# A ternary feed-forward's half chunk packed into one PSUM bank, its slot order, and matmuls put at the head of TensorE's queue, in a four-block float32 network on one core

## The chip, the cores and the metric

The kernel runs on one core of one Trainium2 chip. The metric is device microseconds of one execution. The three runs shown of the kernel before took 422.45, 421.94 and 420.12 us (median 421.94). The profiled execution took 420.34 us, of which the profile's span is 418.6 us.

## The reference

Four residual blocks over 8 sequences of 256 tokens and 256 channels, float32, with a layer norm behind each: a time-mixing recurrence (RWKV), a mixture of 8 experts of which each token takes 2, a linear attention with 16 heads, and a ternary feed-forward. The change touches the last one and the start of the first:

```python
def _quantize(w):                       # w1, w2: (704, 256), w3: (256, 704)
    gamma = jnp.mean(jnp.abs(w))
    return jnp.clip(jnp.round(w / (gamma + EPS)), -1.0, 1.0)
def _bitlinear(x, w): return jnp.matmul(x, _quantize(w).T)
x1 = _bitlinear(x, w1); x2 = _bitlinear(x, w2)
hidden = jax.nn.sigmoid(x1) * x2
return _bitlinear(hidden, w3)
# the first block
k = einsum(xk, Wk); v = einsum(xv, Wv); r = einsum(xr, Wr)
x = layernorm(x + L0_attn(x)); x = layernorm(x + L0_ffn(x))
x = layernorm(x + L1_attn(x)); x = layernorm(x + L1_ffn(x))
```

The hidden width of the last block is 704, which is five and a half chunks of 128.

## The kernel before, in words

All order is written out by hand: each engine has its own list of instructions and waits on semaphores for the others. There are three stages.

Stage A is the recurrence and the routing, sequence by sequence. SyncE issues the loads (`xs[0]`, then `vec`, then `Wk`, `Wv`, `Wr`). ScalarE (L794) and VectorE (L1048) scale the raw weights to `wA`; then TensorE's `project` makes keys, values and gates in float32, of which each instruction appears as two records in the trace (the key projection of a sequence is 8 instructions, 16 records). VectorE's memsets at the head end in `cleared`.

Stage B runs 39 tiles of 128 expert rows. Per tile TensorE does `turn_hidden`, `gate_up` of the tile after the next, `down`, `turn` (L547, L537, L558, L517); VectorE does `hidden_turned` (L1234), on which `down` waits, and `hidden` (L1228). Between them `prepare(i)` slips in one step of other work per tile: the sums of absolute weights (`wsum`, L1298 and L1302), the thresholds, and the quantising of W1, W2 (L1315, L1319) and W3 (L1327 to L1333). `w1q` and `w2q` are padded with zeros to six chunks, and so is `raw3`.

Stage C is attention and the feed-forward, in slots: slot s does the attention of sequence s and the feed-forward of sequence b = s - 1. TensorE's slot for s = 1 to 6 is: `keys_values(s)`, `turn_x3(b)`, `queries(s)`, `key_values(s)`, `ternary(b, 0)`, `attend(s)` (L719), `ternary(b, 1)`, `turn_an(s)`, `ternary_out(b, 0)`, `turn_x2(s+1)`, `ternary(b, 2)`, `attention_out(s)`, `ternary_out(b, 1)`, `ternary_out(b, 2)`. In slot 7 `attention_out` stands ahead of `ternary(b, 2)`, and slot 8 has the feed-forward of the last sequence alone.

A piece p of `ternary` is two chunks: eight matmuls with `w1q` into one bank and eight with `w2q` into another (per chunk two halves of the channels, each with `x3_hi` and `x3_lo`). Each piece then goes ScalarE `tanh_half` (L941), VectorE `gate_times` (L1409), ScalarE `f_high` (`fh`, the rounded high part, L780), VectorE `f_low` (`fl`, what is left, L1415), and back to TensorE's `ternary_out` (L664), eight matmuls into bank 7. Behind the last one VectorE's `block_out` (L1421) takes bank 7, and on the same queue follow its statistics, `combined(s+2)` (L1348, L1351), `keys` (L1426), `x3_low` (L1431), the query limits (L1437), `queries` (L1444) and `mask_kv` (L1450), on which `attend` waits. `attention_residual` (L1472) waits for `attention_out`; behind it come the statistics of `x3` (L1019), GpSimd's `deviation` and ScalarE's `normalise` (L785), for which the next slot's `turn_x3` waits.

## Time and profile before

| | |
|---|---|
| runs | 422.45, 421.94, 420.12 us, median 421.94 |
| the profiled execution | 420.34 us, span 418.6 us |
| TensorE matmuls busy | 378.5 us (90%), 2264 records |
| TensorE weight loads busy | 330.7 us (79%) |
| VectorE busy | 288.5 us (69%) |
| ScalarE busy | 205.2 us (49%) |
| GpSimd busy | 129.7 us (31%) |
| granted TensorE clock, mean | 0.967 |
| chain that ended last | PE 51%, DVE 25%, ACT 10%, issue 6%, POOL 5% |
| stage A / B / C | about 0 to 120 / 120 to 233 / 233 to 418.6 us |

PE is TensorE's matmuls, PEld its weight loads, DVE VectorE, ACT ScalarE, POOL GpSimd, SPq SyncE's queue. Matmuls overlap each other, so their busy time is longer than the time from one start to the next; the starts are to be read for their cost. The chain that ended last is followed back from the last instruction to what released it, or to the instruction before it on its engine. The names in the trace are those of the tiles without their numbers ("arena" is the one large scratch tile).

### The profile page before, as it was taken

The page shows a single profiled execution, that of the slowest core. Times are in us where ns is not written, and L with a number is a line of the kernel's source. Part 1 is how long each engine was busy: PE and PEld are TensorE (multiplying, and loading weights), DVE is VectorE, ACT ScalarE, POOL GpSimd, SP SyncE. Part 2 cuts the span into 40 slices and gives each one's busy share as a digit, 9 for nine tenths or more (in the row PEclk, how much of TensorE's full clock was granted, in tenths as well). Part 3 has the DMA queues.
Part 4 walks back from the last instruction along what each step waited for, and adds up shares of the span by engine and source line. Part 5 has one row for each costly group of instructions (what it writes and reads, how often), then busy time and mean ns, then how long its engine had stood idle before and what let it go on. Part 6 is the DMA issues. An engine that isn't in the chain of part 4 may idle for free.

```text
span 418.6 us, 7345 instructions
## 1 busy us (share of the span) xinstructions
PE 378.5 (90%) x2264; PEld 330.7 (79%) x2264; DVE 288.5 (69%) x756; ACT 205.2 (49%) x419; POOL 129.7 (31%) x228
## 2 busy tenths in 40 slices
PE   3999999999868999999999867999999999999781
PEld 3888888888747877777776757988999999999680
DVE  4697899999984554896453256686868686866531
ACT  3372785568554333355344414545546363646341
POOL 2002166445635500030310377152617131311111
PEclk9999999999978999999999969999999999999886
DMA  6444973421123457533521222101111000000000
GB/s 215 151 167 160 141 191 92 139 76 52 38 76 114 151 178 218 160 104 99 155 74 52 66 78 66 32 28 50 38 39 50 28 27 2 25 2 27 0 27 26
DMA packets 28487, 35.70 MB, mean 85 GB/s; under 512 B 3681, under 2 KB 25633, under 8 KB 28193
## 3 DMA queue, kind: packets, MB, share of 16 engines
q1 hardware_dynamic: 19760, 21.72, 18.3%
q0 software_dynamic: 3072, 8.39, 6.2%
q10 hardware_dynamic: 5616, 5.11, 3.5%
q8 instruction: 20, 0.33, 0.3%
q14 instruction: 19, 0.15, 0.1%
HBM read 22.76 MB, written 12.45 MB: 84 GB/s over the span
## 4 chain that ended last, share of the span: by engine, by line
PE 51%; DVE 25%; ACT 10%; issue 6%; POOL 5%; DMA 1%; SPq 0%; ACTq 0%; POOLq 0%; DVEq 0%
PE bank L394 20%; PE bank L537 11%; PE bank L558 8%; PE bank L664 4%; DVE st L1019 3%; POOL nm L1537 2%; PE bank L719 2%; PE bank L517 2%; PE bank L547 2%; PE bank L404 2%; DVE arena L1080 2%; DVE arena L1444 2%; DVE arena L1083 2%; DVE fl L1415 2%; POOL rs L1534 2%
## 5 line engine op out<-in xcount | busy, mean ns | idle before, releaser
L394 PE MATMUL bank<-arena 128*128 128x256 f32 (+2 forms) x576 | 119.4, 363 | 7.7 <-ACT arena L794 6.4
L394 PEld LDWEIGHTS bank<-arena 128*128 128x128 f32 x576 | 101.8, 194 | 21.5 <-issue 6.4
L780 ACT ACTIVATE arena<-bank 128x256 f32<-128x256 f32 (+1 forms) x118 | 45.4, 423 | 47.3 <-PE bank L558 27.7
L1532 POOL TENSOR_TENSOR ve<-mv,eps 128x2 f32<-128x2 f32 x32 | 7.2, 224 | 157.7 <-DVE mv L1023 157.6
L537 PE MATMUL bank<-gu,arena 128*128 x156 | 54.0, 469 | 0.0
L785 ACT ACTIVATE arena<-arena,nm,rs 128x256 f32<-128x256 f32 x48 | 26.2, 595 | 38.2 <-POOL nm L1537 38.0
L558 PE MATMUL bank<-dn,arena 96*128 x156 | 40.9, 384 | 2.8 <-DVE arena L1234 2.8
L1602 POOL DMA_INDIRECT arena<-yg,ypos x32 | 31.2, 976 | 38.9 <-DMA yg<-arena 30.5
L1234 DVE COPY arena<-bank 96x256 f32<-96x256 f32 x39 | 16.3, 419 | 35.0 <-PE bank L547 34.9
L1574 POOL DMA_INDIRECT xg<-x,pos x32 | 34.3, 1073 | 14.7 <-DVE pos L1143 7.4
L558 PEld LDWEIGHTS bank<-dn,arena 96*128 96x128 f32 x156 | 28.8, 190 | 12.2 <-issue 3.9
L537 PEld LDWEIGHTS bank<-gu,arena 128*128 128x128 f32 x156 | 27.1, 194 | 8.7 <-issue 0.7
L664 PE MATMUL bank<-w3q,fh 128*128 128x256 f32 x96 | 27.2, 315 | 5.2 <-DVE fl L1415 5.2
L1409 DVE SCALAR_TENSOR_TENSOR arena<-arena,bank 128x512 f32<-128x512 f32 x24 | 16.5, 688 | 18.5 <-ACT arena L941 18.5
L941 ACT ACTIVATE arena<-bank 128x512 f32<-128x512 f32 x24 | 14.3, 597 | 29.1 <-PE bank L394 29.1
L394 PE MATMUL bank<-x_hi,w1q 128*128 128x256 f32 x96 | 26.5, 308 | 1.6 <-ACT x_hi L780 1.6
L868 ACT ACTIVATE arena<-bank 128x176 f32<-128x176 f32 x39 | 12.3, 315 | 31.4 <-PE bank L537 31.4
L1537 POOL TENSOR_SCALAR nm<-mv,rs 128x1 f32<-128x1 f32 x64 | 23.8, 385 | 3.2
L1534 POOL TENSOR_TENSOR rs<-ve,neghalf 128x2 f32<-128x2 f32 x32 | 24.0, 751 | 2.5
L394 PE MATMUL bank<-x_lo,w1q 128*128 128x256 f32 x96 | 24.5, 287 | 0.0
L664 PE MATMUL bank<-w3q,fl 128*128 128x256 f32 x96 | 24.4, 286 | 0.0
L394 PE MATMUL bank<-x_hi,w2q 128*128 128x256 f32 x96 | 24.3, 285 | 0.0
(211 smaller groups left out, 855.5 us busy)
## 6 DMA issues: line engine op xcount, KB each, us to landing
arena<-xg SPq DMA_DIRECT2D x39, 128.0 KB, 2.2
yg<-arena ACTq DMA_DIRECT2D x39, 128.0 KB, 1.7
arena<-in_xT SPq DMA_DIRECT2D x8, 256.0 KB, 3.0
x<-in_x SPq DMA_DIRECT2D x8, 256.0 KB, 4.4
out<-arena SPq DMA_DIRECT2D x8, 256.0 KB, 2.1
gu<-in_w_gate SPq DMA_DIRECT2D x1, 1408.0 KB, 7.9
gu<-in_w_up SPq DMA_DIRECT2D x1, 1408.0 KB, 7.7
dn<-in_w_down SPq DMA_DIRECT2D x11, 128.0 KB, 6.1
```

The source lines that it names most:

```text
L394: last = pe.matmul(dst, l, r, start=i == 0, stop=i == len(pairs) - 1)
L537: last = pe.matmul(bank[BANK_GU[i % 2]][:, 0:2 * F], xtT[:, i % 2, chunk(k)], w[:, :, k, :, bass.ds(e, 1), :], start=k == 0, stop=k == KC - 1)
L558: last = pe.matmul(bank[BANK_Y][:, 0:C], hT[0:HALF, i % 2, q, :], dn[0:HALF, q, bass.ds(e, 1), :], start=q == 0, stop=q == 1)
L664: last = pe.matmul(halves(7)[:, t, :], l[:, n % 2, i, chunk(t)], w3q[:, f, :], start=f == 0 and t == 0 and q == 0, stop=f == NF - 1 and q ...
L780: return act.activation(dst, src, ACT.Copy)
L785: last = act.activation(dst[:, t, :], src[:, t, :], ACT.Identity, bias=nm[:, i, t:t + 1], scale=rs[:, i, t:t + 1])
L1234: dve.tensor_copy(hT[0:HALF, i % 2, :, :], bank[BANK_HT][0:HALF, 0:2 * P].rearrange("p (q t) -> p q t", q=2)).then_inc(hT_ok, 1)
L1409: dve.scalar_tensor_tensor(fb[n % 2][:, :, :], fb[n % 2][:, :, :], 1.0, halves(ternary_banks(b, p)[1]), ALU.add, ALU.mult).then_inc(fx_ok, 1)
L1534: pool.tensor_tensor(rs[:, i, :], ve[:, i, :], neghalf[:, :], ALU.pow).then_inc(dev_step, 1)
L1537: last = pool.tensor_scalar(nm[:, i, t:t + 1], mv[:, i, t, 0:1], rs[:, i, t:t + 1], -1.0, ALU.mult, ALU.mult)
L1574: pool.indirect_dma_start(out=xg, out_offset=bass.IndirectOffsetOnAxis(ap=pos[:, n, j:j + 1], axis=0), in_=x1[:, n, :], in_offset=None).th ...
L1602: pool.indirect_dma_start(out=yy[b % 2][:, t, j, :], out_offset=None, in_=source, in_offset=bass.IndirectOffsetOnAxis(ap=ypos[:, n, j:j + ...
```

## The change

- The last piece of `ternary` is split in two. The half chunk (64 gate columns of W1 and the 64 columns of W2 that belong to them) is packed in one set of 128 columns, chunk 5 of `w1q`: four matmuls into one bank (`HALF_PIECE`), where it took eight. Chunk 4 is the piece behind it (`LAST_PIECE`), eight matmuls. ScalarE's tanh of the half piece reads partitions 0 to 63 and writes 64 to 127; its low part is written to partitions 0 to 63 of `fh`, beside the high part, and W3's last 64 rows are loaded twice, so that `ternary_out` needs two matmuls for the half chunk, where it took four.
- The half piece goes to bank 2 (bank 4 for the last sequence) and waits for `gate_times` of piece 1; the last chunk's piece keeps banks 5 and 6.
- ScalarE does tanh, tanh, high, high and VectorE gate, gate, low, low for the two. On VectorE both `f_low` stand ahead of `attention_residual` in slots 1 to 6; before, `f_low` stood behind it.
- `ternary_out` of the half chunk waits for its own low part, and chunk 4 for its own.
- The quantising of W2 writes 640 columns to `w2q` and 64 to `w1q`; the sum over W3 is two instructions, of partitions 0 to 63 with six chunks and of 64 to 127 with five. The memsets of padding are gone.
- At the head: nine float32 matmuls of `ones` by `ones` once `cleared` is there; VectorE's memset of `ones` comes first; `Wk` is the first load on SyncE's queue and `vec` is loaded from ScalarE's.

The diff, cut to its core:

```diff
@@ ternary_banks @@
+    if p == HALF_PIECE:
+        return (4 if b == B - 1 else 2,)
+    return (0, 1) if p == LAST_PIECE and b == B - 1 else (5, 6)
@@ sync @@
+            sp.dma_start(raw_kvr[:, 0, :, :], chunked(Wk)).then_inc(in_kvr[0], 16)
             sp.dma_start(xs[0][:, :, 1:], xT_v[0]).then_inc(in_xsb[0], 16)
-            sp.dma_start(vec[:, :, :], vecs).then_inc(in_vec, 16)
-            for j, w in enumerate((Wk, Wv, Wr)):
+            for j, w in ((1, Wv), (2, Wr)):
@@ tensor @@
+            pe.wait_ge(cleared, 1)
+            for i in range(WARM):
+                pe.matmul(bank[7][:, 0:P], ones[:, :], ones[:, :], start=True, stop=True)
@@ ternary @@
-                past(pe, fx_ok, NPAIR * b + p - 1)
+                if p < HALF_PIECE:
+                    past(pe, fx_ok, PIECES * b)
+                if p == HALF_PIECE and b < B - 1:
+                    pe.wait_ge(fx_ok, PIECES * b + 2)
+                if p == LAST_PIECE and b < B - 1:
+                    pe.wait_ge(fx_ok, PIECES * b + 1)
@@ ternary_out @@
+                groups = [(PIECES * b + p + 1, [(2 * p, 0, (fh, fl)), (2 * p + 1, 1, (fh, fl))])] if p < NPAIR - 1 else [
+                    (PIECES * b + HALF_PIECE + 1, [(NF - 1, 1, (fh,))]),
+                    (PIECES * b + LAST_PIECE + 1, [(NF - 2, 0, (fh, fl))])]
@@ f_low @@
+                low, whole, high = {
+                    HALF_PIECE: (fh[0:LEFT, 0, 1, :], fb[0][LEFT:P, 1, :], fh[LEFT:P, 0, 1, :]),
+                    LAST_PIECE: (fl[:, 0, 0, :], fb[0][:, 0, :], fh[:, 0, 0, :]),
@@ vector, prepare @@
+                    for parts, n in ((slice(0, LEFT), NF), (slice(LEFT, P), NF - 1)):
+                        last = dve.tensor_reduce(wsum[parts, 2:3], raw3[parts, 0:n, :], mybir.AxisListType.XY, ALU.add,
@@ vector, c_slot @@
                 if ffn:
-                    gate_times(s - 1, 2)
+                    gate_times(s - 1, HALF_PIECE)
+                    gate_times(s - 1, LAST_PIECE)
+                    f_low(s - 1, HALF_PIECE)
+                    f_low(s - 1, LAST_PIECE)
                 if s < B - 1:
                     attention_residual(s)
-                if ffn:
-                    f_low(s - 1, 2)
```

TensorE's queue in slots 1 to 6, from the transposes of `turn_x2` to the first matmul of `attention_out` (bank 0). Before:

```order
L404 MATMUL bank4<-cst,arena 128x128 x4
L394 MATMUL bank5<-x3_hi,w1q 128x256
L394 MATMUL bank5<-x3_lo,w1q 128x256
...
L394 MATMUL bank6<-x3_hi,w2q 128x256
L394 MATMUL bank6<-x3_lo,w2q 128x256
...
L394 MATMUL bank0<-biases,pick 128x256
```

After:

```order
L410 MATMUL bank4<-cst,arena 128x128 x4
L400 MATMUL bank2<-x3_hi,w1q 128x256
L400 MATMUL bank2<-x3_lo,w1q 128x256
...
L400 MATMUL bank5<-x3_hi,w1q 128x256
L400 MATMUL bank5<-x3_lo,w1q 128x256
...
L400 MATMUL bank6<-x3_hi,w2q 128x256
L400 MATMUL bank6<-x3_lo,w2q 128x256
...
L400 MATMUL bank0<-biases,pick 128x256
```

There were eight matmuls into bank 5 and eight into bank 6; now there are four into bank 2, four into bank 5 and four into bank 6.

VectorE's queue in the same place (`arena<-arena,bank` is a gate, `fl<-arena,fh` a low part, `arena<-bank0,arena` the residual of attention). Before:

```order
L1415 TENSOR_TENSOR fl<-arena,fh 128x512
L1358 TENSOR_TENSOR xT_lo<-bank4,xT_hi 128x512
L1409 SCALAR_TENSOR_TENSOR arena<-arena,bank6 128x512
L1472 TENSOR_TENSOR arena<-bank0,arena 128x512
L1415 TENSOR_TENSOR fl<-arena,fh 128x512
L1019 BN_STATS st<-arena 128x6 x2
```

After:

```order
L1390 TENSOR_TENSOR xT_lo<-bank4,xT_hi 128x512
L1445 SCALAR_TENSOR_TENSOR arena<-arena,bank2 64x256
L1445 SCALAR_TENSOR_TENSOR arena<-arena,bank6 128x256
L1453 TENSOR_TENSOR fh<-arena,fh 64x256
L1453 TENSOR_TENSOR fl<-arena,fh 128x256
L1509 TENSOR_TENSOR arena<-bank0,arena 128x512
L1047 BN_STATS st<-arena 128x6 x2
```

One gate and one low part of 512 columns became two and two of 256, and all four stand ahead of the residual, which stood between them.

The head of SyncE's queue (`arena<-in_xT` is `xs`). Before:

```order
L315 DMA arena<-in_xT 128x2x256
L316 DMA vec<-in_vecs 128x12
L318 DMA raw_kvr<-in_Wk 128x2x256
L318 DMA raw_kvr<-in_Wv 128x2x256
L318 DMA raw_kvr<-in_Wr 128x2x256
```

After:

```order
L321 DMA raw_kvr<-in_Wk 128x2x256
L322 DMA arena<-in_xT 128x2x256
L324 DMA raw_kvr<-in_Wv 128x2x256
L324 DMA raw_kvr<-in_Wr 128x2x256
L325 DMA arena<-in_xT 128x2x256
```

`Wk` moved from the third place to the first, and `vec` left the queue.

## Rows read from the trace of the kernel before

**Rows 1.** Chain that ended last: start us, duration us, what ran.

```profile
302.93 1.19 PE bank L719 x8
...
307.91 3.87 PE bank L394 x26
...
311.81 0.08 DVE arena L1472
...
312.42 0.69 DVE fl L1415
...
313.15 1.23 PE bank L664 x8
...
314.40 0.70 DVE arena L1421
...
363.11 1.19 PE bank L719 x8
...
382.69 1.19 PE bank L719 x8
```

**Rows 2.** Timeline of slot 3: start us, duration us, engine, line, operation, [idle before].

```profile
306.68 0.69 DVE L1409 SCALAR_TENSOR_TENSOR arena<-arena,bank 128x512 f32<-128x512 f32 x1 [0.49 <-ACT arena L941]
...
307.87 0.28 PE L394 MATMUL bank<-x_lo,w1q 128*128 128x256 f32 x1
...
309.52 0.28 PE L394 MATMUL bank<-x_lo,w2q 128*128 128x256 f32 x1
...
309.84 0.60 ACT L941 ACTIVATE arena<-bank 128x512 f32<-128x512 f32 x1 [1.29 <-PE bank L394]
...
312.44 0.28 PE L664 MATMUL bank<-w3q,fl 128*128 128x256 f32 x1
...
313.02 0.74 DVE L1019 BATCH_NORM_STATS2 st<-arena 128x6 f32<-128x256 f32 x2
```

**Rows 3.** Groups of instructions by line and form: busy us, mean ns.

```profile
L780 ACT ACTIVATE arena<-bank 128x256 f32<-128x256 f32 x94 | 31.2, 380 | 31.4 <-PE bank L558 27.7 <-PE bank L517 3.3 <-PE bank L394 0.4
...
L780 ACT ACTIVATE fh<-arena 128x512 fp32r<-128x512 f32 x24 | 15.1, 628 | 10.3 <-DVE arena L1409 10.3
...
L1464 DVE TENSOR_TENSOR arena<-bank,arena 128x256 f32<-128x256 f32 x16 | 6.0, 420 | 0.3
```

**Rows 4.** Timeline of two places in stage B.

```profile
157.12 1.74 DVE L1302 TENSOR_REDUCE wsum<-raw 128x1 f32<-128x1536 f32 x1
...
160.01 1.03 PE L558 MATMUL bank<-dn,arena 96*128 x4
...
186.58 1.20 DVE L1285 TENSOR_TENSOR slot_a<-slot_a,done_of 128x32 f32<-128x32 f32 x1
...
188.25 1.12 PE L558 MATMUL bank<-dn,arena 96*128 x4 [0.47 <-DVE arena L1234]
```

**Rows 5.** Head: two of the chain, one line's load, matmul durations (min/median/max) in two windows.

```profile
1.81 3.41 DMA raw_kvr<-in_Wk
...
6.40 28.91 PE bank L394 x120
...
L315 SPq DMA_DIRECT2D arena<-in_xT x1: 455/455/455, 0.8 to 0.8; - x1
...
DMA to landing us min/median/max: 2.6/2.6/2.6
...
L394 PE MATMUL bank<-arena x6: 544/634/634, 9.5 to 11.7; 128*128 128x256 f32 x6
...
L394 PE MATMUL bank<-arena x11: 377/378/379, 13.8 to 15.9; 128*128 128x256 f32 x11
```

**Rows 6.** The end: timeline, chain, and the windows view (busy us by engine, PEclk, DMA share).

```profile
393.04 1.07 ACT L785 ACTIVATE arena<-arena,nm,rs 128x256 f32<-128x256 f32 x2
...
398.18 3.44 PE bank L394 x16
...
395.00:400.00 5.00, 3.38 (x16) 3.01 (x15) 2.27 (x6) 1.40 (x3) 1.39 (x4) 0.50 0.00 0
```

More of the change, by code:

```diff
@@ L740, in c_slot @@
                     turn_x3(b)
-                    for p in range(NPAIR):
+                    for p in range(PIECES):
                         ternary(b, p)
@@ L763, in c_slot @@
                 if s:
-                    ternary(b, 2)
+                    ternary(b, HALF_PIECE)
+                    ternary(b, LAST_PIECE)
                 if s < B - 1:
@@ L1024, in statistics @@
                 last.then_inc(mv_ok[i], 1)
+            dve.memset(ones[:, :], 1.0)
             dve.memset(kS[:, :, 0:1], LOW)
```

117 lines of the change are left out of this document (65 added, 52 removed).

## The prediction

> **What bounds the kernel now.** I read the chain of waits first, because the shares of busy time mislead here: TensorE counts as busy for nine tenths of the span, but its matmuls overlap. In slot 3 of stage C the ternary matmuls have 284 ns each as a duration, while fourteen starts lie between 307.87 and 309.52 us, 0.118 us each [rows 2]. So a float32r matmul that goes is worth 0.118 us, and only where TensorE is the one waited for.
>
> The chain shows a slot of stage C as a ring of two parts [rows 1]. From `attend` at 302.93 TensorE is released by itself until `attention_out` is through; then VectorE's residual comes (311.81), then `f_low` of piece 2 (312.42), on which the last `ternary_out` waits (313.15). From the end of that one VectorE goes alone, from `block_out` at 314.40 through the combine, keys and query limits to the mask, on which the next `attend` waits. Three slots later `attend` stands at 363.11, so a slot takes 20.06 us. Whatever ends the last `ternary_out` sooner shortens the ring, as long as the residual and its statistics follow. The last step, from slot 6 to slot 7, takes 19.58 us (363.11 to 382.69).
>
> Stage A starts when `Wk` has landed (issued 1.81, 3.41 us on its way) and the scaled weights let TensorE begin at 6.40. From there the chain has 120 records of TensorE in 28.91 us, so a gain at the head is handed on in full [rows 5]. The end goes over `normalise` of `x3`, the transposes and the feed-forward of the last sequence [rows 6].
>
> **The change part by part.**
>
> *Slots 1 to 6.* I keep the clock of slot 3, whose piece 2 starts two records ahead of 307.87, at 307.67. The half piece is four matmuls, the last chunk eight. Four fewer than 16 end the piece 0.47 us sooner: the last start is 309.05 instead of 309.52. The half piece has a new wait, for `gate_times` of piece 1. That ends at 306.68 + 0.69 = 307.37 [rows 2], 0.3 us ahead, so I cost it at nothing; if the cover goes, `attention_out` and both remaining `ternary_out` queue behind it.
>
> Next I follow the two pieces. ScalarE starts 0.32 us after the start of a piece's last matmul (309.52 to 309.84 [rows 2]): for the last chunk 309.37. A 256-column operation out of PSUM takes 0.38 us on ScalarE and 0.42 on VectorE; 512 columns take 0.69 on VectorE [rows 1] and 0.63 on ScalarE from SBUF [rows 3], so I take 0.42 for a 256-column high part, which no row shows. Then, with 0.03 between engines: tanh 309.37 to 309.75, gate 309.78 to 310.20, high 310.23 to 310.65, low 310.69 to 311.11. The half piece's four steps run in the gaps of these; it may push the high part by about 0.05. The half piece saves nothing by having 64 partitions.
>
> `attention_out` starts 0.47 us sooner, so the residual can start at 311.81 - 0.47 = 311.34 [rows 1]. Both low parts are then ready at about 311.15: 0.2 us of slack. The statistics, which stood behind `f_low` at 313.02 [rows 2], move to about 311.96: 1.06 us sooner. The first pair of chunks of the remaining `ternary_out` is no longer followed by a wait: before, TensorE stood still from 312.44 + 0.12 = 312.56 [rows 2] to 313.15, 0.59 us. And the last group has six matmuls instead of eight, 0.24 us. The first step after the pause goes too: the eight took 1.23 us [rows 1], while seven steps and one duration make 7 x 0.118 + 0.28 = 1.11, so 0.12. Together 0.47 + 0.59 + 0.24 + 0.12 = 1.42. Bank 7 is then ready at 314.40 - 1.42 = 312.98 and VectorE is free for `block_out` at 314.05 - 1.06 = 312.99 (the statistics and their 0.25 us of aggregation end there now): what is late next is VectorE itself, and a slot gains 1.4 us. From there its chain is unchanged. Five slots give 7.0; the step to slot 7 has no combine and goes over `normalise`, so it gets the shift of the statistics, 1.06. Sum **8.1 us**. Bounds: if a 256-column operation costs as much as the 512-column one, the low part is ready about 0.9 us later, the residual 0.7 us late, and a slot keeps 0.67, 4.0 us in all; above, 6 x 1.43 = 8.6.
>
> *Slot 7 to the last ternary.* Here `attention_out` comes first, and the path is `normalise`, which ended at 393.04 + 1.07 = 394.11 [rows 6] because it stood behind the high part. The short chain is through before the scale factors arrive, so `normalise` can start some 0.35 us sooner, and the transposes no longer stand behind eight matmuls at the low clock. Following transposes, high and low part, and `block_out` in front of the latter, I get the first ternary matmul at about 396.1 instead of 398.18: **2.1 us**. The granted clock is 0.50 over 395 to 400, the 1.2 GHz level, and the 16 matmuls took 3.44 us where they take 1.9 at 2.4 GHz [rows 6]. TensorE stands idle here in either kernel, so I leave the clock as it was. Bounds 0.5 (another group of 16 at the low clock) and 3.6 (none).
>
> *Tail.* In slot 8 VectorE and ScalarE alternate over the pieces. The last low part was the end of three chains of 512-column steps; two pairs of 256-column steps that interleave end about 0.36 us sooner, and behind the last wait stand four matmuls instead of eight, 0.47 us: **0.8 us** (0.1 with 512-column prices, 1.0).
>
> *Head, the loads.* `Wk` leaves 1.81 - 0.80 = 1.01 us sooner, and the first load of the queue landed 2.6 us after its issue [rows 5], so it can be there at 3.4 instead of 5.22. Then `xs` (about 4.7, from its issue at 1.31 with `Wk`'s 3.41) and VectorE's part of `wA`, behind its memsets, are next. Gain **1.2 us**, between 0.8 and 1.8.
>
> *Head, the warming.* TensorE's records of 256 columns take 634 ns between 9.5 and 11.7 us, 6 of them 0.43 apart, and 378 ns between 13.8 and 15.9, 11 of them 0.21 apart [rows 5]. The two spacings are those of 1.2 and 2.4 GHz; the column of the granted clock has full speed in both. From 6.40 to 11.7 at 0.43 there are about 13 slow records: 13 x 0.21 = 2.7 us. Nine float32 matmuls of 128 columns are 18 records of half the length, 18 x 0.21 = 3.8 us, from about 1.3 to 5.1, and the real work starts at about 5.2. TensorE has then been at work without a pause before the place where it had worked for some 5.4 us when the clock rose. I take the whole **2.7 us**; the ends are 0 (the clock does not rise on them) and 2.7. Nothing waits behind them that is ready sooner.
>
> The Trainium skill, "TensorE: Matmul & The Clock Gate", section "What's actually happening", speaks against the full sum: it says that the same kernel shows 6, 11 or 14 slow matmuls depending on the moment of its start. By it a run with 6 slow ones would give back an estimated 1.3 us, and the median gain would be lower than this one execution's. Only one execution's trace is here, so no row decides it.
>
> *Sum over W3.* The one reduction of 1.74 us over 1536 columns [rows 4] becomes two, of 1536 and 1280: 1.74 + 1.45 = 3.2 us from 157.12, until 160.3, on VectorE, ahead of `hidden_turned`. A row shows what follows: the long steps until 187.78 let `down` start at 188.25, 0.47 us later. So `down` would start at 160.8 where it stood at 160.01: a loss of **0.8 us** (0.6 to 1.1). The extra 64-column quantising steps, some 0.2 us in each of two tiles, lie in VectorE's idle time there, and the memsets that go were beside loads.
>
> **Sum.** 8.1 + 2.1 + 0.8 + 1.2 + 2.7 - 0.8 = 14.1 us. Against the profiled execution's 420.34 that is 406.2; the median of the three runs stands 1.6 us higher (421.94), and what differs between executions is in part the slow stretches that go. I take 407.0 us, between 406.2 and 407.8.
>
> **The rivals.**
>
> *The clock does not rise on the warming.* The nine matmuls end, and the clock rises as late as before. For it: a group of waiting TensorE at the end of the program runs slow again after a pause [rows 6]. Against it: the work at the head has no pause. Then 407.0 + 2.7 = 409.7 us.
>
> *The residual becomes the late one.* In slots 1 to 6 both low parts stand ahead of it with only 0.2 us of slack; it delays statistics, `normalise` and `block_out`. It decides from 0.2 us of lateness; with the 512-column price it costs 0.7 x 6 = 4.2, and with the tail's 0.7 gives 407.0 + 4.9 = 411.9 us. Against it: every row shows a 256-column step well under its 512-column one.
>
> *The new wait of the half piece,* the one that could end slower than before. `gate_times` of piece 1 has 0.3 us to spare in slot 3; if VectorE comes x later, all of TensorE's slot behind it moves by x - 0.3. To eat the whole gain, 421.94 - 407.0 = 14.9 us in six slots, x must be above 14.9 / 6 + 0.3 = 2.8 us. At 3 us it is 407.0 + 6 x 2.7 = 423.2 us. Nothing in the rows makes VectorE late there.
>
> **How the numbers follow.** Forecast 0.68; no rise of the clock 0.15; late residual 0.12; the new wait 0.02; the rest 0.03 for a gain that is larger (the last ternary at the high clock, 1.5 us more). The range takes in the first three: 403.8 to 412.3 us. One measurement of this kernel tells about 0.5%, 2.1 us, from no change. Faster by over 0.5%: 0.96; within: 0.02; slower: 0.02.
>
> **What would show it.** Right: `attend` every 18.7 us in slots 1 to 6; no idle of TensorE ahead of the last `ternary_out`; statistics of `x3` directly behind the residual, the residual released by TensorE and not by a low part; records 0.21 apart from the first real matmul at about 5.2 us; one `down` about 0.8 us late behind the two reductions. Wrong: a slot of over 19.3 us (a 256-column step is dear), records 0.42 apart past 6 us (no warming), or a pause of TensorE ahead of the first matmuls into bank 2 (the new wait). A longer time with all these in place would be the slow clock elsewhere, at the start of stage B, in slot 0 or in slot 8.

## The result and the profile after

The changed kernel took 410.69 us, the median of four runs (410.51 to 412.06), against 422.19 for the kernel before beside it: a ratio of 0.9746, with a 95% interval of 0.9718 to 0.9773. The gain is 11.5 us. Measured again on another chip, beside the last three experiments, it was 7.7 us (414.15 against 421.82, ratio 0.981, 0.9778 to 0.9842). The two intervals do not overlap, and a good part of this section and the next is about why. The first of the two times lies in the forecast range of 403.8 to 412.3 us, the second lies above it.

| | before, profiled | before, profiled again | after, profiled | after, profiled again |
|---|---|---|---|---|
| time / span, us | 420.34 / 418.6 | 422.48 / 420.7 | 410.51 / 408.6 | 414.08 / 412.2 |
| first residual of stage A | 35.34 | 34.70 | 30.97 | 32.24 |
| ScalarE's 4th to 12th silu of stage B | 22.37 | 24.84 | 23.91 | 26.56 |
| `attend(1)` | 262.79 | 264.83 | 261.10 | 264.55 |
| `attend(1)` to `attend(7)` | 119.90 | 121.91 | 114.02 | 114.08 |
| `attend(7)` to the end of the span | 35.92 | 34.00 | 33.51 | 33.53 |

First the chain that ended last, of the changed kernel, in slot 3 and at `attend(4)`, `attend(6)` and `attend(7)` (start us, duration us, what); it answers to [rows 1]:

```profile
299.42 1.19 PE bank L736 x8
...
308.32 0.70 DVE arena L1509
...
310.08 0.62 DVE arena L1458
...
318.57 1.19 PE bank L736 x8
...
356.44 1.19 PE bank L736 x8
...
375.12 1.19 PE bank L736 x8
```

`f_low` (L1453) and the last `ternary_out` have left the chain. It goes from the attention's residual (L1509) through VectorE alone to `block_out` (L1458), as the prediction had it. But here `attend` comes every 19.15 us, and the forecast 18.7 are only met from `attend(5)` on. The timeline of the same slot, GpSimd, ScalarE and VectorE, answers to [rows 2]:

```profile
301.17 0.95 POOL L1638 DMA_INDIRECT arena<-yg,ypos  x1 [0.30 <-issue]
...
303.04 0.60 ACT L964 ACTIVATE arena<-bank 128x512 f32<-128x512 f32 x1 [1.71 <-PE bank L400]
...
306.36 0.38 ACT L964 ACTIVATE arena<-bank 128x256 f32<-128x256 f32 x1 [0.42 <-PE bank L400]
...
306.38 0.88 DVE L1445 SCALAR_TENSOR_TENSOR arena<-arena,bank 64x256 f32<-64x256 f32 x2
...
307.29 0.42 DVE L1453 TENSOR_TENSOR fh<-arena,fh 64x256 fp32r<-64x256 f32 x1
307.74 0.42 DVE L1453 TENSOR_TENSOR fl<-arena,fh 128x256 fp32r<-128x256 f32 x1
308.32 0.69 DVE L1509 TENSOR_TENSOR arena<-bank,arena 128x512 f32<-128x512 f32 x1 [0.15 <-PE bank L400]
309.05 0.75 DVE L1047 BATCH_NORM_STATS2 st<-arena 128x6 f32<-128x256 f32 x2
```

Both low parts are through at 308.16, and the residual is released by TensorE 0.16 us later; its statistics stand directly behind it. The 64-partition step costs 0.42 us like the 128-partition one. The one row that disagrees is ScalarE's second tanh, at 303.04. TensorE's last matmul of that piece starts 302.24, and in the slots of `attend(5)` and `attend(6)` ScalarE starts 0.32 us after it. Here it is 0.80. This tanh comes 3.13 us after `attend` in the profile of before, and 3.62 in the slots of `attend(2)` to `attend(4)` of the changed kernel.

The head, from the chain of the changed kernel; it answers to [rows 5]:

```profile
1.18 3.61 PE bank L515 x18
4.79 26.16 PE bank L400 x120
...
30.97 0.70 DVE x L1175
```

The same 120 records take 26.16 us instead of 28.91, and start at 4.79 instead of 6.40. The first line is the warming. The same three places of the changed kernel, profiled again:

```profile
1.18 4.21 PE bank L515 x18
5.39 26.82 PE bank L400 x120
32.24 0.70 DVE x L1175
```

This execution reaches the residual 1.27 us later with the same program. The starts tell why: a warming record is 0.21 us from the next at 1.2 GHz and 0.11 at 2.4. In the first profile the spacing falls to 0.11 within the warming, at about 4.1 us. In the second all of the warming is 0.21 apart, and the first four real records, of twice the columns, are 0.43 to 0.52 apart, until about 7.0 us.

Stage B, around the divided sum over W3 (L1330), answers to [rows 4]. `down` is L568, `hidden_turned` L1261:

```profile
154.02 3.23 DVE L1330 TENSOR_REDUCE wsum<-raw 64x1 f32<-64x1536 f32 x2
...
157.28 0.42 DVE L1261 COPY arena<-bank 96x256 f32<-96x256 f32 x1
...
157.84 0.91 PE L568 MATMUL bank<-dn,arena 96*128 x3 [0.78 <-DVE arena L1261]
```

The end, in the chain and the windows view (busy us by engine, PEclk, DMA share, GB/s), answers to [rows 6]:

```profile
385.97 0.59 ACT arena L803
...
388.73 5.56 PE bank L400 x32
```

```profile
385.00:390.00 5.00, 3.02 (x20) 2.45 (x21) 2.68 (x7) 2.11 (x4) 1.82 (x5) 0.97 0.01 2
390.00:395.00 5.00, 5.00 (x32) 5.00 (x32) 1.44 (x3) 2.50 (x5) 0.00 (x0) 0.69 0.15 52
395.00:400.00 5.00, 4.06 (x28) 3.28 (x27) 3.35 (x7) 2.22 (x5) 0.00 (x0) 1.00 0.00 0
```

The stretch at 1.2 GHz is still there, and shorter: a granted clock of 0.69 in one window of 5 us, where it was 0.93, 0.50 and 0.89 in three that follow each other (from 390 to 405 us).

So the sum of the spans against the first profile of before is: head -4.4, another -0.2 by the fourth silu, +1.5 over the eight tiles behind it, +1.0 at the divided sum, +0.5 some eighteen tiles later, -0.1 until `attend(1)`, then -5.9 in the slots and -2.4 at the end, -10.0 in all. Three of these were not in the prediction: the +1.5, the +0.5, and the 0.49 us in each of three slots. At the first two places ScalarE and VectorE are both late and no row shows what for. The experiments had to say whether they belong to the change.

### The profile page after: what moved, and what is told of

Same layout as the page of the kernel before. It is cut to its first block, busy times and chain, and to the rows that moved or that the text cites. A ratio compares the mean times of both kernels' runs of the same rounds, so it can differ in the third digit from the quotient of the medians.

```text
span 408.6 us, 7333 instructions
## 1 busy us (share of the span) xinstructions
PE 373.9 (92%) x2234; PEld 325.4 (80%) x2234; DVE 293.4 (72%) x774; ACT 208.7 (51%) x435; POOL 129.6 (32%) x226
## 4 chain that ended last, share of the span: by engine, by line
PE 47%; DVE 28%; ACT 8%; issue 7%; POOL 7%; DMA 1%; SPq 0%; ACTq 0%; POOLq 0%; DVEq 0%
PE bank L400 18%; PE bank L547 10%; PE bank L568 8%; DVE st L1047 4%; POOL arena L1638 3%; POOL nm L1575 2%; PE bank L527 2%; PE bank L557 2%; PE bank L736 2%; DVE arena L1107 2%; PE bank L410 2%; DVE arena L1110 2%; POOL rs L1572 2%; DVE arena L1481 2%; ACT arena L798 1%
## 5 line engine op out<-in xcount | busy, mean ns | idle before, releaser
L400 PE MATMUL bank<-arena 128*128 128x256 f32 (+2 forms) x576 | 116.6, 357 | 1.7 <-issue 0.7
L400 PEld LDWEIGHTS bank<-arena 128*128 128x128 f32 x576 | 99.8, 190 | 14.8 <-DVE arena L1463 2.0
L568 PE MATMUL bank<-dn,arena 96*128 x156 | 41.1, 386 | 4.6 <-DVE arena L1261 3.8
L1261 DVE COPY arena<-bank 96x256 f32<-96x256 f32 x39 | 16.3, 419 | 36.1 <-PE bank L557 32.6
L568 PEld LDWEIGHTS bank<-dn,arena 96*128 96x128 f32 x156 | 28.6, 190 | 14.8 <-issue 6.9
L964 ACT ACTIVATE arena<-bank 128x512 f32<-128x512 f32 (+2 forms) x32 | 15.6, 488 | 25.0 <-PE bank L400 21.4
L400 PE MATMUL bank<-x_hi,w1q 128*128 128x256 f32 x96 | 26.5, 307 | 1.5 <-ACT x_hi L798 1.5
L1445 DVE SCALAR_TENSOR_TENSOR arena<-arena,bank 128x512 f32<-128x512 f32 (+2 forms) x32 | 17.8, 556 | 12.5 <-ACT arena L964 12.0
L681 PE MATMUL bank<-w3q,fh 128*128 128x256 f32 x96 | 24.2, 305 | 1.4 <-DVE fh L1453 0.8
L1572 POOL TENSOR_TENSOR rs<-ve,neghalf 128x2 f32<-128x2 f32 x32 | 23.9, 748 | 2.5
L803 ACT ACTIVATE x<-x,nm,rs 128x256 f32<-128x256 f32 x16 | 8.7, 592 | 28.1 <-POOL nm L1575 28.1
L400 PE MATMUL bank<-x_lo,w2q 128*128 128x256 f32 x80 | 20.7, 288 | 0.0
```

The source lines that it names most:

```text
L400: last = pe.matmul(dst, l, r, start=i == 0, stop=i == len(pairs) - 1)
L568: last = pe.matmul(bank[BANK_Y][:, 0:C], hT[0:HALF, i % 2, q, :], dn[0:HALF, q, bass.ds(e, 1), :], start=q == 0, stop=q == 1)
L681: last = pe.matmul(halves(7)[:, t, :], l[:, p % 2, i, chunk(t)], w3q[:, f, :], start=f == 0 and t == 0 and q == 0, stop=f == NF - 2 and q ...
L803: last = act.activation(dst[:, t, :], src[:, t, :], ACT.Identity, bias=nm[:, i, t:t + 1], scale=rs[:, i, t:t + 1])
L1445: dve.scalar_tensor_tensor(f, f, 1.0, times, ALU.add, ALU.mult).then_inc(fx_ok, 1)
L1572: pool.tensor_tensor(rs[:, i, :], ve[:, i, :], neghalf[:, :], ALU.pow).then_inc(dev_step, 1)
```

## The experiments

There were twelve runs, two of them of the kernel before and the changed kernel once more, in three sets of four; each set ran on one chip, beside the kernel before. The three chips differ, so times are compared within a set, and across sets only as ratios to the kernel before. The steps of `attend` in us, from the traces, serve for most of them:

| | 1 to 2 | 2 to 3 | 3 to 4 | 4 to 5 | 5 to 6 | 6 to 7 |
|---|---|---|---|---|---|---|
| before | 20.07 | 20.07 | 20.05 | 20.06 | 20.07 | 19.58 |
| before_again | 20.32 | 20.66 | 20.61 | 20.64 | 20.10 | 19.58 |
| head_only | 20.08 | 20.52 | 20.55 | 20.53 | 20.09 | 19.57 |
| after | 19.16 | 19.16 | 19.15 | 19.15 | 18.72 | 18.68 |
| after_again | 18.97 | 19.25 | 19.25 | 19.21 | 18.71 | 18.69 |
| pack_only | 19.02 | 19.10 | 19.10 | 19.17 | 18.74 | 18.69 |
| no_slot_gathers | 18.98 | 18.74 | 18.71 | 18.72 | 18.70 | 18.67 |
| gathers_later | 18.97 | 18.73 | 18.71 | 18.71 | 18.72 | 18.68 |
| half_twice | 19.48 | 19.68 | 19.70 | 19.76 | 19.19 | 19.17 |
| low_late | 19.76 | 20.04 | 19.99 | 19.95 | 19.49 | 19.45 |

### The two halves of the change

The packing alone, with the old head:

```diff
-            sp.dma_start(raw_kvr[:, 0, :, :], chunked(Wk)).then_inc(in_kvr[0], 16)
             sp.dma_start(xs[0][:, :, 1:], xT_v[0]).then_inc(in_xsb[0], 16)
-            for j, w in ((1, Wv), (2, Wr)):
+            sp.dma_start(vec[:, :, :], vecs).then_inc(in_vec, 16)
+            for j, w in enumerate((Wk, Wv, Wr)):
...
-            for i in range(WARM):
-                pe.matmul(bank[7][:, 0:P], ones[:, :], ones[:, :], start=True, stop=True)
```

> The changed kernel with the head of the kernel before (the old order of loads, no warming matmuls), so the packing alone, with the split reduction of W3. By the first theory (the parts add up) it gives the slots and the end without the head: attend(1) to attend(7) 114.0 us (119.9 before), attend(7) to the end of the span 33.5 (35.9), about -8.3, and stage B loses 1.0 to the split reduction of W3 in tile 9; about -7.3, a ratio of 0.983, 415 us. By the rival (the three places in stage B where ScalarE and VectorE stand still together, 2.0 us, come with the packing and its other instruction stream) it loses these too: 417 us, 0.988. Slots 2 to 4 each with 0.49 us between the end of TensorE's second piece and ScalarE's tanh, or without.

It took 414.23 us against 422.05, ratio 0.983 (0.979 to 0.986): a gain of 7.8 us, near the 415 of the first theory, with 113.8 us from `attend(1)` to `attend(7)` and 33.5 from there to the end. The head alone, added to the kernel before:

```diff
+            sp.dma_start(raw_kvr[:, 0, :, :], chunked(Wk)).then_inc(in_kvr[0], 16)
             sp.dma_start(xs[0][:, :, 1:], xT_v[0]).then_inc(in_xsb[0], 16)
...
+            for i in range(WARM):
+                pe.matmul(bank[7][:, 0:P], ones[:, :], ones[:, :], start=True, stop=True)
```

> The kernel before with the new head alone (Wk first, the vectors by ScalarE's queue, nine warming matmuls). First theory: the 4.4 us gained by the start of stage B stay, and no reduction is split: 417.8 us against 422.2, a ratio of 0.990. Rival: a gain at the head moves the times at which the loads of stage B land against the work and brings the joint standstills of ScalarE and VectorE (2.0 us) by itself: 419.8, 0.994, with attend(1) 2.4 us earlier instead of 4.4. The slots stay at 20.06 us.

It took 416.87 us, ratio 0.990 (0.987 to 0.993): a gain of 5.2 us. The two gains add up to 13.0, more than the 11.5 and 7.7 of the whole change on two other chips; the whole change did not run in this set. The slots show more than the times, and did not stay at 20.06 us as expected: without any packing, three of them are 0.46 us longer than in the profile of before, and the tanh of those slots is late by the same amount. Each half of the change has it without the other, so it belongs to neither alone.

### The parts of the head

> The changed kernel without the nine warming matmuls, else the same. First theory: TensorE's clock rises after the real work has begun, the first residual of stage A comes 2.7 us later, and the whole kernel 2.7 us later than the changed kernel: 413.4. Rival: the later start is taken up by waits in stage A and B that end on loads or on VectorE: 411.5 or less.

> The changed kernel with the old order of loads (x first, then the vectors, then Wk, all on SyncE's queue), the warming kept. First theory (the gain of the loads was 1.6 us by the trace, first real matmul at 4.8 instead of 6.4): 412.3 us, first real matmul at 6.4, and the clock still high when it comes, since the warming ends at 4.8 and 1.6 us of rest follow. Rival: the clock falls in that rest, the first matmuls run at the lower clock and the loss is up to 2.7 us larger: 415.

With their edits (the warming loop left out; the old order of loads) they took 412.64 and 411.79 us, on the same chip as the two above. Four heads on one chip, then, read from the chains, first without and then with warming; the last is head_only:

| | loads | first real matmul | 120 records | first residual |
|---|---|---|---|---|
| pack_only | old | 6.78 | 28.15 | 34.96 |
| no_warm | new | 5.54 | 28.62 | 34.18 |
| old_loads | old | 5.81 | 26.21 | 32.04 |
| head_only | new | 5.30 | 25.98 | 31.31 |

Between pack_only and old_loads, which differ by the warming, the first residual moves by 2.9 us (34.96 to 32.04) and the time by 2.4 (414.23 to 411.79). Between pack_only and no_warm, which differ by the loads, it is 0.8 (34.96 to 34.18) and 1.6 (414.23 to 412.64). These are single profiles and medians of four; the times of old_loads alone spread from 409.99 to 413.67. And the 2.9 are not all the warming's. `Wk`, in the chain first of pack_only and then of old_loads, with the same order of loads:

```profile
1.81 3.79 DMA raw_kvr<-in_Wk
```

```profile
1.81 2.81 DMA raw_kvr<-in_Wk
```

The load took 1.0 us less in the second execution, and the real work began 1.0 us sooner for it. The 120 records, which are what the warming is to shorten, took 1.9 us less (28.15 to 26.21).

no_warm lies between its two theories (413.4 and 411.5). Its real work starts 1.24 us sooner than that of pack_only, but eleven of its records are at the 1.2 GHz spacing instead of nine, and that takes back 0.5.

What the head gives is not handed on one for one either. By the fourth silu of stage B the same four stand at 136.90, 136.55, 132.90 and 132.11 us: there old_loads is 4.0 us ahead of pack_only, and no_warm 0.4. A stretch of lower clock lies in between, and it is placed otherwise in the two warmed profiles (old_loads has 0.67, 0.84 and 0.80 in the three windows from 110 to 125 us, pack_only has 0.50 from 120 to 125 and 0.81 in the next).

old_loads was to test whether the clock falls in a rest of 1.6 us between the warming and the real work. That rest did not come about: the warming ends at 5.39 and the real work begins at 5.81, 0.42 us later, and the warming's records are all 0.21 apart, so that the clock had not risen yet. It stands at 2.4 GHz from the second real record on, so a rest of 0.42 us did not keep it from rising. Whether it falls in a longer one was not tested. The time of 411.79 us is that of the first theory (412.3) and not of the rival (415), but it does not decide between them.

### The kernel before, profiled again

> The kernel before, profiled once more. Of its eleven times so far two lie at 420.0 and 420.2 beside the profiled 420.3, and the others between 421.7 and 422.7. First theory: the profiled execution of before lacked standstills that most executions have (ScalarE's second tanh of a slot 0.46 to 0.5 us late in the slots of attend 2 to 4, and about 1.6 us around tiles 4 to 7 of stage B), and this profile shows some of them: a time of 422 with slot periods of 20.5 in three slots, or silu of tile 7 at 151.8 instead of 150.25. Rival: the standstills belong to the changed program; then this profile is like the first, 20.06 in every slot, whatever the time.

422.48 us, and all of the standstills are there: steps of 20.6 us in three slots, the eight tiles in 24.84 us instead of 22.37, and 0.6 us more about eighteen tiles later. The rows around the second tanh of the slot of `attend` at 305.81, ScalarE and GpSimd of the kernel before, profiled again:

```profile
307.57 0.95 POOL L1602 DMA_INDIRECT arena<-yg,ypos  x1 [0.30 <-issue]
...
309.50 0.60 ACT L941 ACTIVATE arena<-bank 128x512 f32<-128x512 f32 x1 [1.77 <-PE bank L394]
```

The tanh starts 3.69 us after `attend`, where it was 3.12 in the first profile. So the first profile, on which the whole prediction rests, was an execution without standstills. Of the eight times measured for before beside the first set, two lie at 420.0 and 420.2 us and six between 421.7 and 422.7. The changed kernel has to be held against this second profile: slots 121.91 to 114.02, 7.9 us; until `attend(1)` 3.7; the end 0.5, while this execution had no stretch at 1.2 GHz in its last sequence. Together 12.1 us of span.

### Whose standstill it is

```diff
-                if s + 3 < B:
-                    gather(s + 3)
```

The edit leaves out the gathers for sequences 3 to 7. VectorE's wait for them is edited too: it combines the rows of sequences 1 and 2 in their place.

> The changed kernel without the five gathers that GpSimd issues during the slots (sequences 3 to 7 are combined from rows gathered for sequences 1 and 2; the gathers, 4 instructions of 0.95 us each, and their 2.6 MB are left out). First theory: the late tanh of three slots and the wait of 0.3 us ahead of the combination in the slot before come with these gathers; without them all slots up to the sixth take 18.70 us: attend(1) to attend(5) 74.8 instead of 76.6, and the kernel 408.9 instead of 410.7. Rival: the standstill is not theirs; the slots stay at 19.15 and the time within 0.3 us of the changed kernel's.

The late tanh is gone; the slots take 18.7 us, as expected, except the first (18.98). The total, 411.07 us and a ratio of 0.973 (0.970 to 0.976), is above the expected 408.9; the profiled execution took 26.56 us for the eight tiles of stage B, which lie ahead of everything that was edited. So the standstill of the slots is shown to need the gathers where they stand. They are not enough for it: the first profile of before has the same gathers at the same distance from `attend`, and no standstill. In all ten profiles that have it, and in the same three slots of each, it ends 1.80 to 1.98 us after the start of the fourth of GpSimd's four indirect DMAs (301.17 to 303.04 above, 307.57 to 309.50 in before_again).

Then the gathers were kept and moved:

```diff
                 if s + 3 < B:
+                    pool.wait_ge(an_ok, s + 1)
                     gather(s + 3)
```

> The changed kernel with a wait in GpSimd's program: the four gathers of a slot begin when the attention's division is done (2.7 us after attend) instead of 2.0 us before attend. They then run to about 7.5 us after attend, where GpSimd is idle until 10.4 anyway, and their rows are needed a slot later. First theory (a standstill of all signals of about 0.5 us comes 1.4 to 1.9 us after the fourth gather begins): it moves to 7.9 to 8.4 after attend, where VectorE works on parts that are already ready and only TensorE's wait at 9.2 follows, and costs little: slots of 18.75 instead of 19.15 in three slots, 409.3 us. Rival: the standstill falls on the chain wherever it is put: 19.15 or more stay, 410.7.

The rows of gathers_later in the slot of `attend` at 299.61; the fourth gather now starts at 306.62:

```profile
302.56 1.25 POOL L1638 DMA_INDIRECT arena<-yg,ypos  x1 [5.22 <-DVE arena L1501]
...
302.74 0.60 ACT L964 ACTIVATE arena<-bank 128x512 f32<-128x512 f32 x1 [1.22 <-PE bank L400]
...
306.62 0.95 POOL L1638 DMA_INDIRECT arena<-yg,ypos  x1 [0.30 <-issue]
...
308.06 0.69 DVE L1509 TENSOR_TENSOR arena<-bank,arena 128x512 f32<-128x512 f32 x1 [0.20 <-issue]
```

The tanh stands at 3.13 us again and the slots take 18.71 to 18.73 us, 1.6 us less over three slots than after_again. The time was 413.11 (410.62 to 413.72), ratio 0.979 (0.975 to 0.982), beside 414.15 for the changed kernel: 1.0 us better in the median, with intervals that overlap. The slots show the gain; the times alone do not prove it. From `attend(7)` to the end the profile has 34.4 us instead of 33.5, and both_fixes has 34.7, so part of the gain is lost there to a longer stretch at the lower clock (0.66 in both windows from 385 to 395 us in gathers_later; after_again has 0.77 from 390 to 395 and 0.89 in the next); whether the later gathers have to do with that is open.

The expectation was that the standstill moves to where nobody waits. The traces do not show that it is still there: in the slots of `attend(1)` to `attend(6)` every instruction of TensorE, VectorE and ScalarE starts within 0.05 us of its place in no_slot_gathers, counted from `attend`. Either it falls where nothing waits or it does not come at all.

What stands still for half a microsecond is not settled. The trace records TensorE's signal for the piece at 303.02, 0.50 us after the modelled end of its last matmul, although TensorE's next instructions start on time, so it is the signal that is late and not the work. The Trainium skill, "NOTIFIC — the notification-queue block", section "7.1 Overflow: three behaviours, one of which stalls the engine", describes a notification path that can hold back an engine; no run here can show whether it is at work, and an execution without the profiler cannot be seen.

### The eight tiles of stage B, and the changed kernel again

> The changed kernel, unchanged, beside the three below. 410.7 us by its four times so far, with a profile in which silu of tile 7 and attend(1) say how much this execution stood still in stage B, and periods of 19.15 in the slots of attend 2 to 4 if the standstill after the gathers is in this execution too. First theory (they come in most executions of every version): both are there, and the ratio is 0.972 to 0.977. Rival: periods of 18.70 throughout.

Its time was 414.15 us (412.87 to 414.35). The slots are those of the first profile, and so is the end. Of the 3.5 us of span between the two profiles 1.27 are there at the first residual, of which 0.5 are left by the fourth silu of stage B (133.66 instead of 133.20), and 2.65 come in the eight tiles behind it, 26.56 us instead of 23.91. VectorE, TensorE and GpSimd of after_again there:

```profile
143.27 0.96 POOL L1610 DMA_INDIRECT xg<-x,pos  x1 [0.30 <-issue]
...
145.23 0.42 DVE L1261 COPY arena<-bank 96x256 f32<-96x256 f32 x1 [2.94 <-remote]
...
145.79 1.13 PE L568 MATMUL bank<-dn,arena 96*128 x4 [1.62 <-DVE arena L1261]
...
147.44 2.55 PE L547 MATMUL bank<-gu,arena 128*128 x4
```

and its windows, with the granted clock in the third column from the right:

```profile
140.00:145.00 5.00, 4.18 (x22) 3.05 (x20) 1.70 (x8) 1.47 (x5) 3.32 (x4) 1.00 0.55 188
145.00:150.00 5.00, 4.21 (x13) 3.02 (x14) 1.45 (x5) 0.99 (x3) 0.00 (x0) 0.69 0.45 158
```

Again the standstill ends 1.96 us after the start of a fourth indirect DMA, here of the scatter (1.9 to 2.0 in ten of the profiles; in after, head_only and old_loads it is shorter and ends 1.1 to 1.2 after). TensorE stands for 1.62 us, then the granted clock falls to the lower level for a part of the window, and the four matmuls of `gate_up` take 2.55 us where they take 1.35 at 2.4 GHz. The profiles fall into three kinds by these eight tiles: 22.4 us without standstills (the first profile of before); 23.9 to 24.8 with them (before_again, after, pack_only, head_only, no_warm, old_loads, gathers_later); and 26.5 with them and the lower clock behind them (after_again, no_slot_gathers, w3_by_columns, low_late, half_twice and both_fixes). The mean granted clock was 0.964 in all six executions of after_again and 0.969 to 0.973 in the four of the first measurement. That all six lost their time at this place is a reading of that mean, not shown for each. That the scatters cause the standstill was not tried; only its place behind them is seen.

Nor does the length of the pause decide whether the clock falls. GpSimd, VectorE and TensorE of gathers_later at the same place:

```profile
142.34 0.96 POOL L1610 DMA_INDIRECT xg<-x,pos  x1 [0.30 <-issue]
...
144.36 0.42 DVE L1261 COPY arena<-bank 96x256 f32<-96x256 f32 x1 [2.98 <-remote]
...
144.92 1.13 PE L568 MATMUL bank<-dn,arena 96*128 x4 [1.67 <-DVE arena L1261]
```

TensorE stands for 1.67 us here, and for 1.54 to 1.58 in pack_only, no_warm and before_again, and the clock stays up in all four. What else it depends on, no run separates. Against these the lower clock costs 2.3 to 2.4 us (26.5 against 24.1 to 24.2, and 1.7 against before_again's 24.84). With two profiles of before, one of them with such a pause, it is not shown that before is spared: two of its eleven runs beside after_again took 423.5 and 424.3 us at a mean granted clock of 0.968 and 0.969.

### The terms of the slot

One saving of TensorE taken back, by computing the half piece twice:

```diff
-                for w, dst in zip((w1q, w2q), ternary_banks(b, p)):
+                dsts = ternary_banks(b, p)
+                for w, dst in zip((w1q, w2q), dsts) if len(dsts) == 2 else ((w1q, dsts[0]), (w1q, dsts[0])):
```

> The changed kernel with the four matmuls of the half piece computed twice (the packing's saving of four matmuls a slot taken back, 4 of 0.12 us each at the full clock, all else kept). First theory (the attention's residual ends the wait on TensorE in each slot, so that each matmul ahead of it counts): the residual starts at 8.95 instead of 8.47 us after attend, each of six slots is 0.48 us longer, and the kernel is 2.9 to 3.3 us slower, 413.8. Rival: VectorE is the bound there and takes up 0.2 us or more of each: 412.5 or less.

Each step is longer by 0.43 to 0.55 us (18.69 to 19.17 in the last), and the sum of the six by 2.9 (114.08 to 116.98). So four matmuls ahead of the residual are worth 0.48 us a slot, as costed. The time was 415.36 us (412.94 to 416.64) beside 414.15, 1.2 us more where 2.9 was expected; the spread of this kernel's runs is larger than the difference, and I take the slots for the answer.

And the order of VectorE's two low parts and the residual:

```diff
-                    f_low(s - 1, HALF_PIECE)
-                    f_low(s - 1, LAST_PIECE)
                 if s < B - 1:
                     attention_residual(s)
+                if ffn:
+                    f_low(s - 1, HALF_PIECE)
+                    f_low(s - 1, LAST_PIECE)
```

> The changed kernel with VectorE's low parts of the half piece and of the last piece behind the attention's residual instead of ahead of it. First theory (the packing pays only if both low parts are ready when TensorE reaches them): the last group of ternary_out, at 9.3 us after attend, then waits until 9.6 (half piece) and 10.0 (last piece), block_out and all behind it come about 0.5 us later, +0.5 in each of six slots: 413.7. Rival: VectorE is the bound and only its order changes, since statistics fill the time until TensorE ends: 411.0 or less.

418.06 us, ratio 0.989 (0.986 to 0.991): 6.4 to 7.0 us worse than the two other changed kernels of its set, more than the 3 that the expectation gave; the six steps are 4.3 us longer than those of w3_by_columns in the same set (118.68 against 114.37), and the end 2.6 (34.69 against 32.09, which had no lower clock there). VectorE of low_late behind an `attend` at 302.82:

```profile
311.80 0.69 DVE L1509 TENSOR_TENSOR arena<-bank,arena 128x512 f32<-128x512 f32 x1 [1.06 <-PE bank L400]
312.52 0.42 DVE L1453 TENSOR_TENSOR fh<-arena,fh 64x256 fp32r<-64x256 f32 x1
312.97 0.43 DVE L1453 TENSOR_TENSOR fl<-arena,fh 128x256 fp32r<-128x256 f32 x1
313.31 0.75 DVE L1047 BATCH_NORM_STATS2 st<-arena 128x6 f32<-128x256 f32 x2
```

I had costed TensorE's wait for the low parts (0.5 us). What I had left out is VectorE: it stands idle for 1.06 us ahead of the residual, and then has 0.8 us more to do before the statistics. They start 1.51 us after the residual instead of 0.73, and each of the last two steps grew by 0.77. TensorE is late by as much: counted from `attend`, its last matmul of `ternary_out` starts at 11.09 us instead of 10.26, and `block_out` at 11.44 instead of 10.58. So the run shows what VectorE's order costs, and not which of the two ends last. More than half of the slot's gain of 1.4 us is thus that two low parts fit into VectorE's pause ahead of the residual, which they do since they are ready there.

### The sum over W3

```diff
-                    for parts, n in ((slice(0, LEFT), NF), (slice(LEFT, P), NF - 1)):
-                        last = dve.tensor_reduce(wsum[parts, 2:3], raw3[parts, 0:n, :], ...
+                    for parts, col, fs in ((slice(0, P), 2, slice(0, NF - 1)), (slice(0, LEFT), 3, slice(NF - 1, NF))):
+                        last = dve.tensor_reduce(wsum[parts, col:col + 1], raw3[parts, fs, :], ...
```

> The changed kernel with the sum over W3 split by columns instead of by rows: five chunks on all 128 rows, then the half chunk on 64 rows into a column of its own, which one more matmul adds. The first has 1280 elements on each row, the second 256, together 1536 as in the undivided reduction of before, against 1536 and 1280 in the changed kernel. First theory: tile 9 of stage B loses 0.1 to 0.2 us instead of 1.03, and the kernel takes 409.8. Rival: the time saved there is lost again before stage C, where a load or a gather ends last: 410.5 or more.

VectorE of w3_by_columns:

```profile
157.03 1.80 DVE L1332 TENSOR_REDUCE wsum<-raw 128x1 f32<-128x1280 f32 x2
...
158.93 0.42 DVE L1263 COPY arena<-bank 96x256 f32<-96x256 f32 x1
```

The reductions take 1.80 us instead of 3.23, and the tile loses nothing. But ahead of `down` at 162.92, some four us later, the added matmul costs 0.4 us, so 0.6 of 1.03 us are left. The time, 411.69 us with a ratio of 0.974 (0.973 to 0.976), shows nothing of it: the changed kernel did not run in this set, and the profiled execution too had the lower clock in stage B.

> The changed kernel with the later gathers and the sum over W3 split by columns. First theory: the two gains add, 1.4 us in the slots and 0.6 in tile 9 of stage B: 408.7 us, a ratio of 0.968, and less than both kernels. Rival: the standstills of stage B, which differ from execution to execution by 2 us and more, hide the 0.6: the same as with the later gathers alone.

412.33 us (409.02 to 413.81), ratio 0.977 (0.972 to 0.981). It has the best median of its set, 1.8 us under the changed kernel beside it, and is 9.5 us under the kernel before; but its interval overlaps that of after_again, and its profile has the lower clock in stage B (26.5 us) and a longer one at the end (34.75 us). The slots add up as expected, 112.52 us from `attend(1)` to `attend(7)`. That the two edits together are faster than the changed kernel is likely and not proven.

## Why the prediction was right, point by point

**The time.** 407.0 us was forecast, with a range to 412.3; it was 410.7. The sum of 14.1 us was set against an execution that had no standstills and one long stretch at the lower clock in its last sequence. The first made before look fast, the second made it look slow. Between the two first profiles it is 10.0 us of span instead of 14.1: 2.2 less in the slots, 0.5 less at the end, 0.2 less at the sum over W3 and 2.0 lost in stage B, against 0.8 more by `attend(1)` at the head and beside these places. That 410.7 lies in the range is in part luck. The range went up to 412.3 for two rivals, and neither of them occurred; what used that room was the standstills, which no term had. Measured again, the time was 414.15, outside it. The lower end, 403.8, is worked out from no term.

**Slots, 8.1 us: right in mechanism, and near in size once like is held against like.** Against the first profile of before the slots gave 5.9 us. Against before_again, which stands still as the changed kernel does, they gave 7.9. Where neither stands still the step is 18.72 against 20.07, 1.35 for 1.4 forecast, and the six together are 119.90 against 112.51 (no_slot_gathers), 7.4. The parts are confirmed one by one: the four matmuls (half_twice, 0.48 for 0.47), the statistics that follow the residual at once (low_late), the residual released by TensorE with 0.16 us of slack for 0.2, and a 256-column step at 0.38 us on ScalarE out of PSUM and 0.42 on VectorE. The step from slot 6 to 7 gained 0.90 (19.58 to 18.68) for 1.06. In the lower bound a slot keeps 1.42 - 0.7 = 0.72 us, not the 0.67 written; it changes nothing else.

**Slot 7 to the last ternary, 2.1 us, and the tail, 0.8.** From `attend(7)` to the first matmul of the last ternary it is 13.61 us (375.12 to 388.73) instead of 15.49: 1.9. From there to the end of the span 19.90 instead of 20.43: 0.5. Together 2.4 for 2.9. The term that I left alone, the clock, moves more than that: before_again has no lower clock there and ends in 34.00 us, 1.9 less than before with the same program. Against that one the end gained only 0.5; w3_by_columns, which has none either, ends in 32.1, 1.9 less than before_again. Like for like, then, the two terms gave 1.9 us without the lower clock, where 2.9 were forecast.

**Loads, 1.2 us, and warming, 2.7.** The first real matmul came 1.6 us sooner, and the 120 records took 2.75 less: 4.4 for 3.9. In the set of four heads, on one chip, the loads brought the real work 1.2 us forward (6.78 to 5.54) and the warming made the 120 records 1.9 us shorter (28.15 to 26.21). The 2.7 us were a count of slow records in one execution, and that count varies. By the spacing of the starts, before has 13 of them, before_again and no_warm 11, pack_only 9. With warming the real work has none in five profiles (after, head_only, old_loads, gathers_later, low_late), one in no_slot_gathers and both_fixes, three in half_twice and four in after_again and w3_by_columns. This is what the rule of the Trainium skill that I set beside it says ("TensorE: Matmul & The Clock Gate", section "What's actually happening": the number of slow matmuls varies with the moment of the start), and the traces agree as far as the count goes; what it depends on, they do not show. No profile without warming had as few as six. The 120 records take 28.15 to 28.91 us in the four profiles without warming and 25.98 to 26.82 in the ten with it, in the mean 28.6 and 26.3, which makes 2.3 us for the 2.7 forecast. The first profile of after was the best draw of the ten: its first residual, 30.97 us, is the earliest, and 32.24 in after_again the latest.

Two statements beside these terms were too simple. The start of the real work was worked out from the loads; in nine of the ten warmed profiles the chain leads over the warming instead, whose end moves between 4.79 and 5.39 us. And a gain at the head was to be handed on in full: from before to after it is (4.4 at the residual, 4.6 at the fourth silu of stage B), but of the 1.27 us between the two profiles of the changed kernel only 0.5 arrive there.

**Sum over W3, -0.8 us.** It cost 1.03, within the bounds of 0.6 to 1.1. The two reductions are 3.23 us, as worked out (3.2).

**What no step had.** The sum took stage B for a stretch that hands on what the head gives. It loses 2 us there to standstills that before can have too (its second profile has them), and in some executions 2.3 to 2.4 more to the lower clock behind one of them. The lower clock shows there in six of the twelve profiles of changed kernels and in neither of the two of before, which are too few to say that the change brings it. The rivals did not occur: the clock was up when the real work began, or after at most four of its records, the residual was not late, and the half piece's new wait never ended a pause of TensorE.

## What to carry to other kernels

One profiled execution is not the kernel: when a few of its runs lie a half per cent apart, profile it twice before costing a change, and compare executions that have the same standstills and the same stretches of lower clock. In a ring where VectorE is the bound, the work worth moving is what fits into its one pause; that was worth more here (0.77 us a slot) than the four matmuls saved (0.48). And a change at the head has to be followed to the next places where TensorE pauses, since the clock there differs from execution to execution by as much as the head gives.

## What the runs showed of the hardware

- Four indirect DMAs in a row on GpSimd's queue are followed by a standstill of about 0.5 us in three slots of stage C, in ten of the eleven profiles that have them there. It ends 1.8 to 2.0 us after the start of the fourth. Without the gathers it is gone, and with the gathers 5 us later it shows nowhere in the slots. Longer ones (VectorE idle for 2.1 to 3.0 us, TensorE for up to 1.67) follow the scatters in stage B. The first profile of before has neither.
- A pause of TensorE of about 1.6 us in the middle of the kernel was followed by a stretch at 1.2 GHz in six profiles, which cost 2.3 to 2.4 us on top, and by none in four others with pauses of 1.54 to 1.67 us.
- With the same warming from 1.18 us on, the spacing of TensorE's matmuls went over to that of 2.4 GHz between about 4.1 us and 7.2 us, at 4.1 and 7.0 in two profiles of the same kernel.
- A VectorE step of 256 columns takes 0.42 us on 64 partitions as on 128, so a reduction that is split by rows costs nearly twice: 3.23 us against 1.74 undivided, and 1.80 split by columns.
